# Cross-attention scores: probabilities kept as bit patterns, one maximum per half, another order on VectorE

## The chip, the cores and the metric

The kernel runs on one core of a Trainium2 chip. The metric is device time in microseconds (us) of the whole launch, and lower is better. TensorE (PE) multiplies matrices, VectorE (DVE) reduces and copies, ScalarE (ACT) does exponentials and copies, GpSimd (POOL) and SyncE (SP) do the rest. Each engine works through its own list of instructions in order and waits on semaphores that the others raise.

## The reference

One decoder layer on x of 2 x 512 tokens by 512 channels: a causal self-attention, a cross-attention to 2048 context tokens, and a mixture of 8 experts. The change touches the cross-attention, 16 heads of 32 channels, 1024 queries, 2048 keys:

```python
q = _fq_sym(q, axis=-1)
k = _fq_sym(k, axis=-1)
v = _fq_sym(v, axis=2)
attn = jnp.einsum('bhqd,bhkd->bhqk', q, k)
attn = jax.nn.softmax(attn.astype(jnp.float32), axis=-1)
attn = _fq_unsigned(attn, axis=-1)
out = jnp.einsum('bhqk,bhkd->bhqd', attn, v)
```

`_fq_unsigned` rounds every probability to one of 256 steps between 0 and the row's largest. The kernel gets those steps without a division: exp(score - largest score + log 255), rounded to an integer, is the step number, and the sum of the unrounded values gives the softmax's denominator.

## The kernel before, in words

The whole layer is one program of stages. The change is in `cross_scores` (L1178 to L1384 of the printed function) and in the type of one tile that `cross_attention` allocates.

**Units.** The work of `cross_scores` is 128 units: 8 tiles of 128 queries (`TT`) times 16 heads (`H`), head fastest. Unit n has two halves of 1024 keys, a (keys 0 to 1023) and b (keys 1024 to 2047). For each unit:

- TensorE makes the scores of a half with two matmuls of 512 columns (`scores`, L1342) into PSUM: half a into one of two buffers `cs_s_a`, half b into the one buffer `cs_s_b`.
- VectorE takes the maximum: of half a with one reduction over 1024 (`max_a`, L1301), of half b with two over 512, the first as soon as the first matmul is done (L1313). A small reduction over the three results (L1316) and a multiply-add (L1320) give the bias of the exponential, `cs_bias`.
- ScalarE does two exponentials of 1024, half b first, then a (L1287). Each writes 16-bit integers 0 to 255 to `cs_p_int`, and is followed by a short instruction that reads out the sum (ACTIVATION_READ_ACCUMULATOR).
- TensorE transposes each half in 8 blocks of 128 x 128 (L1350) into the one PSUM buffer `cs_tp`, viewing the integers as 16-bit floats. Half b goes first and is copied out by ScalarE (L1293), then half a, which is copied out by VectorE (L1328). Both copies convert the integer to a bf16 number in `cs_pT`.
- TensorE multiplies `cs_pT` by the values `v_int` in 16 matmuls of 32 columns (L1376) into `cs_out`.

**Order of the work.** It is written out by hand as one `step(t, h, n)` for each engine. TensorE's step n is: scores b of unit n (after the exponential b of unit n-1 has read `cs_s_b`), transposes b of n-1, scores a of n+1 (after exponential a of n-1), the value matmuls of n-2, transposes a of n-1. VectorE's step n is: maximum b of n, small maximum, bias of n, maximum a of n+1, copy of the transposed half a of n-1, and once a tile the copy of `cs_out` (L1332). ScalarE's step n is: exponential b, exponential a, copy of the transposed half b, all of n; at a new tile it also keeps the sums (L1270) and fetches the scales (L1280). The first 15 units and the last are unrolled, the 112 between run in a hardware loop of 16 units, seven turns.

**The table.** ScalarE's exponential needs a table. The load (ACT_TABLE_LOAD) stands just before the first exponential, behind that one's wait for the bias.

Of the kernel before, what the change touches and what calls it, by code (L numbers as in the profile page):

```python
# [6 lines left out]
F32 = mybir.dt.float32  # L7
# [25 lines left out]
QMAX = 127.0  # L33
PMAX = 255.0
LN_PMAX = log(PMAX)
Q_FLOOR = 1e-08


# [1138 lines left out]
def cross_scores(nc, k_parts, v_int, q_int, q_step, q_nstep, o_raw, z_sum, wp_dram, bp_dram, wp, ident16):  # L1177
# [10 lines left out]
    with ExitStack() as ctx:  # L1188
# [7 lines left out]
            return ctx.enter_context(nc.semaphore("cs_" + name))  # L1196

        p_int = sb("cs_p_int", [P, 2, KEYS], I16)
        pT = sb("cs_pT", [P, 2, KT, P], BF16)
        top = sb("cs_top", [P, 2, 3], F32)  # L1200
        top1 = sb("cs_top1", [P, 2], F32)


# [1 line left out]
        nstep_now = sb("cs_nstep_now", [P, H], F32)  # L1205
        z_now = sb("cs_z_now", [P, H, 2], F32)
        bias = sb("cs_bias", [P, 2], F32)
        s_a = [psum(f"cs_s_a{i}", [P, HALF], F32) for i in range(2)]
        s_b = psum("cs_s_b", [P, HALF], F32)
        tp = psum("cs_tp", [P, HKT, P], F16)  # L1210
# [55 lines left out]
        @block.scalar  # L1266
        def _(act):
            def keep_sums(t, n):
                act.wait_ge(ea_ok, n)
                nc.scalar.copy(z_sum[:, t, :, :], z_now[:, :, :]).then_inc(act_tile, 1)  # L1270
                act.wait_ge(act_tile, 2 * t + 2)

            def step(t, h, n):
                if not exists(n):
                    return
                u = h % 2
                if h == 0:
                    if at_least(n, H):
                        keep_sums(t - 1, n)
                    nc.scalar.copy(step_now[:, :], q_step[:, t, :]).then_inc(act_tile, 1)  # L1280
                    act.wait_ge(act_tile, 2 * t + 1)
                for half, s, made, used in ((1, s_b, eb_ok, tb_ok), (0, s_a[u], ea_ok, ta_ok)):
                    if half:
                        act.wait_ge(bias_ok, n + 1)
                    if at_least(n, 2):
                        act.wait_ge(used, n - 1)
                    nc.scalar.activation(p_int[:, u, half * HALF:(half + 1) * HALF], s[:, :], ACT.Exp,  # L1287
                                         bias=bias[:, u:u + 1], scale=step_now[:, h:h + 1],
                                         accum_out=z_now[:, h, half:half + 1]).then_inc(made, 1)
                act.wait_ge(tb_ok, n + 1)  # L1290
                if at_least(n, 2):
                    act.wait_ge(av_ok, n - 1)
                nc.scalar.copy(pT[:, u, HKT:KT, :], tp[:, :, :].bitcast(I16)).then_inc(rb_ok, 1)  # L1293
            units(act, step)
            keep_sums(TT - 1, UNITS)

        @block.vector
        def _(v_):
# [4 lines left out]
            def step(t, h, n):  # L1303
                u = h % 2
                if exists(n):
                    if h == 0:
# [1 line left out]
                            v_.wait_ge(bias_ok, n)  # L1308
                        nc.vector.tensor_copy(nstep_now[:, :], q_nstep[:, t, :]).then_inc(dve_tile, 1)
                        v_.wait_ge(dve_tile, t + 1)  # L1310
                    for c in range(2):
                        v_.wait_ge(sb_ok, 2 * n + c + 1)
                        nc.vector.tensor_reduce(top[:, u, 1 + c:2 + c], s_b[:, c * 512:(c + 1) * 512], AX_X,  # L1313
                                                ALU.max).then_inc(max_ok, 1)
                    v_.wait_ge(max_ok, 3 * n + 3)
                    nc.vector.tensor_reduce(top1[:, u:u + 1], top[:, u, :], AX_X, ALU.max).then_inc(top_ok, 1)  # L1316
                    v_.wait_ge(top_ok, n + 1)
                    if at_least(n, 2):
                        v_.wait_ge(ea_ok, n - 1)
                    nc.vector.tensor_scalar(bias[:, u:u + 1], top1[:, u:u + 1], nstep_now[:, h:h + 1], LN_PMAX,  # L1320
                                            ALU.mult, ALU.add).then_inc(bias_ok, 1)
                if exists(n + 1):
                    max_a(1 - u, n + 1)
                if at_least(n, 1) and exists(n - 1):
                    v_.wait_ge(ta_ok, n)
                    if at_least(n, 3):
                        v_.wait_ge(av_ok, n - 2)
                    nc.vector.tensor_copy(pT[:, 1 - u, 0:HKT, :], tp[:, :, :].bitcast(I16)).then_inc(ra_ok, 1)  # L1328
                if h == 1 and at_least(n, H):

                    v_.wait_ge(av_ok, n - 1)
                    nc.vector.tensor_copy(o_raw[:, t - 1, :], out[:, :]).then_inc(out_read, 1)  # L1332

            max_a(0, 0)
            units(v_, step)

        @block.tensor
        def _(pe):
            def scores(t, h, s, half, made, each_bank=False):
                for c in range(2):  # L1340
                    keys = half * HALF + c * 512
                    ins = nc.tensor.matmul(s[:, c * 512:(c + 1) * 512], q_int[0:3 * D, t, h, :],  # L1342
                                           k_parts[0:3 * D, h, keys:keys + 512], start=True, stop=True)
                    if each_bank or c == 1:
                        ins.then_inc(made, 1)

            def transposes(u, half, made):
                for k in range(HKT):
# [4 lines left out]
            def step(t, h, n):  # L1353
                u = h % 2
                before = at_least(n, 1) and exists(n - 1)
                if exists(n):
                    if at_least(n, 1):
                        pe.wait_ge(eb_ok, n)
                    scores(t, h, s_b, 1, sb_ok, each_bank=True)
                if before:  # L1360
                    pe.wait_ge(eb_ok, n)
                    if at_least(n, 2):
# [6 lines left out]
                if at_least(n, 2):  # L1369
# [3 lines left out]
                    if head == 0 and at_least(n, H):  # L1373
                        pe.wait_ge(out_read, t)
                    for k in range(KT):
                        ins = nc.tensor.matmul(out[:, head * D:(head + 1) * D], pT[:, u, k, :],  # L1376
                                               v_int[:, k, head * D:(head + 1) * D], start=(k == 0), stop=(k == KT - 1))
                    ins.then_inc(av_ok, 1)
                if before:
# [134 lines left out]
def cross_attention(nc, wq, bq, ctxT, wkv_in, bkv, wp, bp, v_raw, x_res, mv, rstd, ident, minus_half, ident16, ident_bf, used):  # L1514
    with ExitStack() as ctx:
# [2 lines left out]

        k_parts = sb("k_parts", [3 * D, H, KEYS], BF16)
        v_step = sb("v_step", [P, C], F32)  # L1520
        v_int = sb("v_int", [P, KT, C], BF16)

        wq_raw = v_int[:, :, :].rearrange("p t c -> p (t c)")[:, 0:2 * CK * C].bitcast(F32)\
            .rearrange("p (k c) -> p k c", k=CK)
# [774 lines left out]
```

## Time and profile before

| what | value |
|---|---|
| time, median of 3 runs (lowest, highest) | 1240.04 us (1235.86, 1241.66) |
| time of the profiled execution | 1237.78 us |
| its span in the trace | 1236.1 us |
| busy, share of the span: PE / DVE / ACT / POOL | 81% / 69% / 57% / 20% |
| `cross_scores`, first to last exponential b | 404.6 to 865.1 us |
| largest groups: L1313 DVE, L1301 DVE, L1287 ACT (two), L1350 PE | 164.8, 155.5, 154.1, 152.8, 158.4 us |

The span is from the first to the last instruction of the profiled execution, and the time of that execution is 1.7 us more. A timeline row gives the start of an instruction, its duration, engine, line, operation and tiles; where instructions of one line follow each other they are merged, with their count at the end (x8). An idle time before a row and what ended it stand in brackets. Busy PE includes the time in which a result is still on its way out of the array, so consecutive matmuls overlap in it.

### The profile page before, as it was taken

What the parts mean: (1) busy time and instruction counts of PE and PEld (TensorE: products, weight loads), DVE (VectorE), ACT (ScalarE), POOL (GpSimd) and SP (SyncE); (2) the same over time, 40 slices, a digit from 0 to 9 for tenths busy, and PEclk for the clock granted to TensorE, in tenths of its full rate; (3) what the DMA queues carried; (4) which work ended last, traced back from release to release, by engine and by line L of the source; (5) the groups of instructions that cost most, each with busy time, mean ns of one, the idle gap of its engine ahead of it and who ended that gap; (6) DMA issues with size and microseconds to landing.
All of it is one profiled execution on the core that took longest, in us unless ns stands there. A gap on an engine that the chain in (4) does not pass through costs nothing. (4 is left out here: it accounts for less than half of the span.)

```text
span 1236.1 us, 21867 instructions
## 1 busy us (share of the span) xinstructions
PE 1003.9 (81%) x8049; PEld 682.7 (55%) x8049; DVE 852.8 (69%) x1409; ACT 700.4 (57%) x1039; POOL 243.6 (20%) x216
## 2 busy tenths in 40 slices
PE   4888996999457777777777777777779989999998
PEld 3745744888345444444444444444557765556566
DVE  6857546999687899999999999999661521111126
ACT  3453362455426899999999999999223202212221
POOL 1134063556250200000000000000533610000014
PEclk9999998999678799999999999999779989999999
DMA  8200004110000000000000000000040395131215
GB/s 320 96 1 1 1 2 154 51 34 17 9 0 13 31 1 2 1 0 0 0 0 0 0 0 0 0 0 0 1 151 27 135 379 230 60 116 64 69 56 182
DMA packets 24854, 68.14 MB, mean 55 GB/s; under 512 B 2722, under 2 KB 6818, under 8 KB 23778
## 3 DMA queue, kind: packets, MB, share of 16 engines
q1 hardware_dynamic: 20114, 52.48, 11.3%
q0 software_dynamic: 4400, 14.42, 3.7%
q8 instruction: 35, 0.57, 0.2%
q10 hardware_dynamic: 288, 0.52, 0.1%
q14 instruction: 17, 0.14, 0.0%
HBM read 49.07 MB, written 18.35 MB: 55 GB/s over the span
## 5 line engine op out<-in xcount | busy, mean ns | idle before, releaser
L1313 DVE TENSOR_REDUCE cs_top<-cs_s_b 128x1 f32<-128x512 f32 x256 | 164.8, 685 | 16.7 <-PE cs_s_b L1342 7.6
L1350 PE MATMUL cs_tp<-ident,cs_p_int 128*128 128x128 f16 x2048 | 158.4, 221 | 7.5 <-ACT cs_pT L1293 2.8
L1287 ACT ACTIVATE cs_p_int<-cs_s_b,cs_bias,cs_step_now 128x1024 int16<-128x1024 f32 x128 | 154.1, 1204 | 11.6 <-DVE cs_bias L1320 5.3
L1301 DVE TENSOR_REDUCE cs_top<-cs_s_a 128x1 f32<-128x1024 f32 x128 | 155.5, 1215 | 7.2 <-PE cs_s_a L1342 7.2
L1350 PEld LDWEIGHTS cs_tp<-ident,cs_p_int 128*128 128x128 f16 x2048 | 122.1, 98 | 60.3 <-issue 45.6
L1342 PE MATMUL cs_s_b<-k_parts,q_int 96*128 96x512 bf16 x256 | 79.0, 391 | 93.4 <-ACT cs_p_int L1287 93.1
L1287 ACT ACTIVATE cs_p_int<-cs_s_a,cs_bias,cs_step_now 128x1024 int16<-128x1024 f32 x128 | 152.8, 1194 | 0.0
L1293 ACT CAST cs_pT<-cs_tp 128x1024 bf16<-128x1024 int16 x128 | 129.5, 1012 | 3.3 <-PE cs_tp L1350 2.7
L2159 PE MATMUL ff_h<-ff_experts,ff_zgT 128*128 x368 | 115.1, 467 | 1.0 <-ACT ff_zgT L1798 0.9
L1446 POOL TENSOR_TENSOR co_o<-co_o,v_step 128x512 f32<-128x512 f32 x8 | 10.7, 1331 | 467.6 <-DVE co_o L1468 467.6
L1342 PE MATMUL cs_s_a<-k_parts,q_int 96*128 96x512 bf16 x256 | 79.4, 393 | 22.9 <-ACT cs_p_int L1287 18.7
L1328 DVE CAST cs_pT<-cs_tp 128x1024 bf16<-128x1024 int16 x128 | 87.1, 680 | 4.3 <-PE cs_tp L1350 3.9
L2159 PEld LDWEIGHTS ff_h<-ff_experts,ff_zgT 128*128 128x128 f32 x368 | 69.3, 193 | 36.7 <-issue 3.3
L1376 PEld LDWEIGHTS cs_out<-v_int,cs_pT 128*128 128x128 bf16 x2048 | 70.3, 96 | 31.3 <-issue 1.1
L2052 DVE TENSOR_TENSOR ff_run_g<-ff_run_s,ff_h 128x352 f32<-128x352 f32 x23 | 12.0, 521 | 99.0 <-ACT ff_run_s L1835 82.8
L1342 PEld LDWEIGHTS cs_s_b<-k_parts,q_int 96*128 (+1 forms) x256 | 14.7, 97 | 116.6 <-ACT cs_p_int L1287 109.7
L1376 PE MATMUL cs_out<-v_int,cs_pT 128*128 128x32 bf16 x2048 | 71.4, 177 | 0.8 <-DVE cs_pT L1328 0.8
L2182 PE MATMUL ff_py<-ff_experts,ff_gT 128*128 x138 | 63.2, 593 | 0.8 <-DVE ff_gT L2016 0.8
L1835 ACT ACTIVATE ff_run_s<-ff_h 128x352 f32<-128x352 f32 x23 | 10.7, 464 | 90.4 <-PE ff_h L2159 90.4
L245 POOL TENSOR_TENSOR stage<-stage,mask 128x512 f32<-128x512 f32 x32 | 40.3, 1274 | 61.2 <-ACT stage L316 61.2
L2015 DVE COPY ff_gT<-ff_pc 128x256 f32<-128x256 f32 x23 | 9.8, 424 | 61.1 <-PE ff_pc L2170 61.1
L529 PE MATMUL sa_pj<-sa_w_hi,sa_z_hi 128*128 128x512 f32 x96 | 40.0, 417 | 7.5 <-DVE sa_y L409 3.8
(278 smaller groups left out, 2099.0 us busy)
## 6 DMA issues: line engine op xcount, KB each, us to landing
ff_experts<-in_experts_dram SPq DMA_DIRECT2D x8, 2176.0 KB, 14.6
slots<-sa_zero SPq DMA_DIRECT2D x1, 5888.0 KB, 25.8
ff_zg<-slots POOLq DMA_DIRECT2D x23, 256.0 KB, 2.9
run_y<-ff_yv SPq DMA_DIRECT2D x23, 256.0 KB, 2.0
ff_raw<-in_weights_dram SPq DMA_DIRECT2D x6, 768.0 KB, 5.8
ck_raw<-in_ctxT_dram SPq DMA_DIRECT2D x8, 512.0 KB, 3.3
stage<-in_cwkv_dram SPq DMA_DIRECT2D x2, 1024.0 KB, 6.8
out_dram<-x_res SPq DMA_DIRECT2D x8, 256.0 KB, 2.0
```

What stands on the lines that cost most here:

```text
L245: pool.tensor_tensor(diag, diag, mask[:, :].unsqueeze(1).broadcast_to([P, GH, P]), ALU.mult).then_inc(masked, 1)
L529: ins = nc.tensor.matmul(out, a(k), w[:, m, k, :], start=(k == 0 and i == 0), stop=(k == CK - 1 and i == 2))
L1287: nc.scalar.activation(p_int[:, u, half * HALF:(half + 1) * HALF], s[:, :], ACT.Exp, bias=bias[:, u:u + 1], scale=step_now[:, h:h + 1], ac ...
L1293: nc.scalar.copy(pT[:, u, HKT:KT, :], tp[:, :, :].bitcast(I16)).then_inc(rb_ok, 1)
L1301: nc.vector.tensor_reduce(top[:, u, 0:1], s_a[u][:, :], AX_X, ALU.max).then_inc(max_ok, 1)
L1313: nc.vector.tensor_reduce(top[:, u, 1 + c:2 + c], s_b[:, c * 512:(c + 1) * 512], AX_X, ALU.max).then_inc(max_ok, 1)
L1328: nc.vector.tensor_copy(pT[:, 1 - u, 0:HKT, :], tp[:, :, :].bitcast(I16)).then_inc(ra_ok, 1)
L1342: ins = nc.tensor.matmul(s[:, c * 512:(c + 1) * 512], q_int[0:3 * D, t, h, :], k_parts[0:3 * D, h, keys:keys + 512], start=True, stop=True)
L1350: ins = nc.tensor.transpose(tp[:, k, :], p_int[:, u, key:key + P].bitcast(F16), ident16[:, :])
L1376: ins = nc.tensor.matmul(out[:, head * D:(head + 1) * D], pT[:, u, k, :], v_int[:, k, head * D:(head + 1) * D], start=(k == 0), stop=(k == ...
L2159: ins = nc.tensor.matmul(out[u % 2][:, 0:I_W], zgT[:, u % 2, k, :], w, start=(k == 0), stop=(k == CK - 1))
L2182: ins = nc.tensor.matmul(py[u % 2][:, :], gT[0:rows, u % 2, j, :], w, start=(j == 0), stop=(j == DN - 1))
```

## The change

It touches `cross_scores` in seven places.

1. `cs_pT` holds the 16-bit integers as they are instead of bf16 numbers. The value matmuls view them as half-precision floats (an integer n then reads as n / 2^24), `v_int` becomes half-precision, and the copy of `cs_out` becomes a multiplication by 2^24 (`P_UNIT`).
2. ScalarE's copy of a transposed half views both sides as 32-bit integers: 512 elements instead of 1024. VectorE's copy keeps 1024 elements of 16 bits, without a conversion.
3. The maximum of half b is one reduction over 1024, which waits for both matmuls, and TensorE raises `sb_ok` once a unit.
4. The small maximum is over two numbers.
5. VectorE copies the transposed half a of n-1 before it takes the maximum of half a of n+1, not after.
6. An exponential of one column on a tile of its own stands at the head of ScalarE's list, and the table load with it.
7. The copy of `cs_out` is a `tensor_scalar` in place of a `tensor_copy`.

```diff
+P_UNIT = 2.0 ** 24
...
-        pT = sb("cs_pT", [P, 2, KT, P], BF16)
-        top = sb("cs_top", [P, 2, 3], F32)
+        pT = sb("cs_pT", [P, 2, KT, P], I16)
+        top = sb("cs_top", [P, 2, 2], F32)
...
-                nc.scalar.copy(pT[:, u, HKT:KT, :], tp[:, :, :].bitcast(I16)).then_inc(rb_ok, 1)
+                nc.scalar.copy(pT[:, u, HKT:KT, :].rearrange("p k q -> p (k q)").bitcast(I32),
+                               tp[:, :, :].rearrange("p k q -> p (k q)").bitcast(I32)).then_inc(rb_ok, 1)
+            nc.scalar.activation(table[:, :], ident16[:, 0:1], ACT.Exp)
...
-                    for c in range(2):
-                        v_.wait_ge(sb_ok, 2 * n + c + 1)
-                        nc.vector.tensor_reduce(top[:, u, 1 + c:2 + c], s_b[:, c * 512:(c + 1) * 512], AX_X,
-                                                ALU.max).then_inc(max_ok, 1)
-                    v_.wait_ge(max_ok, 3 * n + 3)
+                    v_.wait_ge(sb_ok, n + 1)
+                    nc.vector.tensor_reduce(top[:, u, 1:2], s_b[:, :], AX_X, ALU.max).then_inc(max_ok, 1)
+                    v_.wait_ge(max_ok, 2 * n + 2)
...
-                if exists(n + 1):
-                    max_a(1 - u, n + 1)
                 if at_least(n, 1) and exists(n - 1):
                     v_.wait_ge(ta_ok, n)
                     if at_least(n, 3):
                         v_.wait_ge(av_ok, n - 2)
                     nc.vector.tensor_copy(pT[:, 1 - u, 0:HKT, :], tp[:, :, :].bitcast(I16)).then_inc(ra_ok, 1)
+                if exists(n + 1):
+                    max_a(1 - u, n + 1)
                 if h == 1 and at_least(n, H):
                     v_.wait_ge(av_ok, n - 1)
-                    nc.vector.tensor_copy(o_raw[:, t - 1, :], out[:, :]).then_inc(out_read, 1)
+                    nc.vector.tensor_scalar(o_raw[:, t - 1, :], out[:, :], P_UNIT, None, ALU.mult).then_inc(out_read, 1)
...
-            def scores(t, h, s, half, made, each_bank=False):
+            def scores(t, h, s, half, made):
...
-                    if each_bank or c == 1:
-                        ins.then_inc(made, 1)
+                ins.then_inc(made, 1)
...
-                        ins = nc.tensor.matmul(out[:, head * D:(head + 1) * D], pT[:, u, k, :],
+                        ins = nc.tensor.matmul(out[:, head * D:(head + 1) * D], pT[:, u, k, :].bitcast(F16),
...
-        v_int = sb("v_int", [P, KT, C], BF16)
+        v_int = sb("v_int", [P, KT, C], F16)
```

VectorE's list in `cross_scores`, one unit in the steady state, before. `cs_s_a` and `cs_s_b` are the scores of the two halves, `cs_tp` the transposed half, and the brackets hold the semaphores that the instruction waits for.

```order
L1301 TENSOR_REDUCE cs_top<-cs_s_a 128x1 [waits cs_sa_ok]
L1328 CAST cs_pT<-cs_tp 128x1024 [waits cs_av_ok,cs_ta_ok]
L1313 TENSOR_REDUCE cs_top<-cs_s_b 128x1 [waits cs_sb_ok] x2
L1316 TENSOR_REDUCE cs_top<-cs_top 128x1 [waits cs_max_ok]
L1320 TENSOR_SCALAR cs_bias<-cs_top,cs_nstep_now 128x1 [waits cs_ea_ok,cs_top_ok]
```

The same place of the changed kernel:

```order
L1322 TENSOR_SCALAR cs_bias<-cs_top,cs_nstep_now 128x1 [waits cs_ea_ok,cs_top_ok]
L1328 COPY cs_pT<-cs_tp 128x1024 [waits cs_av_ok,cs_ta_ok]
L1305 TENSOR_REDUCE cs_top<-cs_s_a 128x1 [waits cs_sa_ok]
L1316 TENSOR_REDUCE cs_top<-cs_s_b 128x1 [waits cs_sb_ok]
L1318 TENSOR_REDUCE cs_top<-cs_top 128x1 [waits cs_max_ok]
```

The copy, with its wait for the transposes of half a (`cs_ta_ok`), now stands right behind the bias and ahead of both maxima of the next unit; the two reductions of half b are one.

ScalarE's list at the head of `cross_scores`, before:

```order
L1280 COPY cs_step_now<-q_step 128x16
L1287 ACT_TABLE_LOAD [waits cs_bias_ok]
L1287 ACTIVATE cs_p_int,cs_z_now<-cs_s_b,cs_bias,cs_step_now 128x1024 [waits cs_act_tile]
L1287 ACTIVATE cs_p_int,cs_z_now<-cs_s_a,cs_bias,cs_step_now 128x1024
L1293 CAST cs_pT<-cs_tp 128x1024 [waits cs_tb_ok]
```

And of the changed kernel:

```order
L1297 ACT_TABLE_LOAD
L1297 ACTIVATE cs_table<-ident 128x1
L1282 COPY cs_step_now<-q_step 128x16
L1289 ACTIVATE cs_p_int,cs_z_now<-cs_s_b,cs_bias,cs_step_now 128x1024 [waits cs_bias_ok,cs_act_tile]
L1289 ACTIVATE cs_p_int,cs_z_now<-cs_s_a,cs_bias,cs_step_now 128x1024
L1295 COPY cs_pT<-cs_tp 128x512 [waits cs_tb_ok]
```

The table load has moved ahead of the wait for the first bias, and the copy has half as many elements.

## Rows read from the trace of the kernel before

**Rows 1.** Window 404.5 to 865: length, busy PE, PEld, DVE, ACT, POOL, granted clock, DMA.

```profile
404.50:865.00 460.50, 343.77 (x4546) 218.69 (x4546) 432.66 (x774) 444.71 (x650) 6.40 (x2) 0.99 0.00 0
```

**Rows 2.** Timeline, one unit and its neighbours: start us, us, engine, line, operation.

```profile
499.19 1.21 DVE L1301 TENSOR_REDUCE cs_top<-cs_s_a 128x1 f32<-128x1024 f32 x1
499.31 1.20 ACT L1287 ACTIVATE cs_p_int<-cs_s_b,cs_bias,cs_step_now 128x1024 int16<-128x1024 f32 x1
500.32 0.68 DVE L1328 CAST cs_pT<-cs_tp 128x1024 bf16<-128x1024 int16 x1
500.41 0.19 ACT L1287 ACTIVATION_READ_ACCUMULATOR cs_p_int<-cs_s_b,cs_bias,cs_step_now 128x1 f32 x1
500.50 1.19 ACT L1287 ACTIVATE cs_p_int<-cs_s_a,cs_bias,cs_step_now 128x1024 int16<-128x1024 f32 x1
500.66 0.60 PE L1342 MATMUL cs_s_b<-k_parts,q_int 96*128 96x512 bf16 x2 [0.64 <-ACT cs_p_int L1287]
501.08 1.29 DVE L1313 TENSOR_REDUCE cs_top<-cs_s_b 128x1 f32<-128x512 f32 x2
501.14 0.61 PE L1350 MATMUL cs_tp<-ident,cs_p_int 128*128 128x128 f16 x8
501.79 1.01 ACT L1293 CAST cs_pT<-cs_tp 128x1024 bf16<-128x1024 int16 x1
501.93 0.60 PE L1342 MATMUL cs_s_a<-k_parts,q_int 96*128 96x512 bf16 x2 [0.18 <-ACT cs_p_int L1287]
502.37 0.56 PE L1376 MATMUL cs_out<-v_int,cs_pT 128*128 128x32 bf16 x16
502.41 0.16 DVE L1316 TENSOR_REDUCE cs_top<-cs_top 128x1 f32<-128x3 f32 x1
502.60 0.21 DVE L1320 TENSOR_SCALAR cs_bias<-cs_top,cs_nstep_now 128x1 f32<-128x1 f32 x1
502.73 1.21 DVE L1301 TENSOR_REDUCE cs_top<-cs_s_a 128x1 f32<-128x1024 f32 x1
502.85 1.20 ACT L1287 ACTIVATE cs_p_int<-cs_s_b,cs_bias,cs_step_now 128x1024 int16<-128x1024 f32 x1
502.94 0.61 PE L1350 MATMUL cs_tp<-ident,cs_p_int 128*128 128x128 f16 x8
```

**Rows 3.** Groups of instructions: count, busy us, mean ns of one, idle before it.

```profile
L1313 DVE TENSOR_REDUCE cs_top<-cs_s_b 128x1 f32<-128x512 f32 x256 | 164.8, 685 | 16.7 <-PE cs_s_b L1342 7.6
L1301 DVE TENSOR_REDUCE cs_top<-cs_s_a 128x1 f32<-128x1024 f32 x128 | 155.5, 1215 | 7.2 <-PE cs_s_a L1342 7.2
L1328 DVE CAST cs_pT<-cs_tp 128x1024 bf16<-128x1024 int16 x128 | 87.1, 680 | 4.3 <-PE cs_tp L1350 3.9
L2015 DVE COPY ff_gT<-ff_pc 128x256 f32<-128x256 f32 x23 | 9.8, 424 | 61.1 <-PE ff_pc L2170 61.1
L1293 ACT CAST cs_pT<-cs_tp 128x1024 bf16<-128x1024 int16 x128 | 129.5, 1012 | 3.3 <-PE cs_tp L1350 2.7
L1798 ACT COPY ff_zgT<-ff_pc 128x512 f32<-128x512 f32 x23 | 13.5, 585 | 37.7 <-PE ff_pc L2147 37.7
```

**Rows 4.** Instructions of L1287: durations ns, then first and last start us.

```profile
L1287 ACT ACTIVATE cs_p_int<-cs_s_b,cs_bias,cs_step_now x128: 1203/1203/1211, 404.6 to 865.1; 128x1024 int16<-128x1024 f32 x128
```

**Rows 5.** Timeline at the stage's start, ScalarE.

```profile
403.26 1.28 ACT L1287 ACT_TABLE_LOAD   x1 [4.03 <-DVE cs_bias L1320]
```

**Rows 6.** Timeline, VectorE, two instructions that follow with no gap.

```profile
642.56 0.68 DVE L1332 COPY stage<-cs_out 128x512 f32 x1
643.16 0.68 DVE L1313 TENSOR_REDUCE cs_top<-cs_s_b 128x1 f32<-128x512 f32 x1
```

**Rows 7.** Timeline near the stage's start, ScalarE, first exponential of two consecutive units.

```profile
408.74 1.21 ACT L1287 ACTIVATE cs_p_int<-cs_s_b,cs_bias,cs_step_now 128x1024 int16<-128x1024 f32 x1
412.92 1.21 ACT L1287 ACTIVATE cs_p_int<-cs_s_b,cs_bias,cs_step_now 128x1024 int16<-128x1024 f32 x1
```

**Rows 8.** Window 408 to 412, same columns as Rows 1; granted clock 0.50.

```profile
408.00:412.00 4.00, 3.56 (x21) 1.99 (x20) 3.42 (x6) 3.22 (x5) 3.32 (x1) 0.50 0.00 0
```

More of the change, by code:

```diff
@@ L1207, in cross_scores @@
         bias = sb("cs_bias", [P, 2], F32)
+        table = sb("cs_table", [P, 1], F32)
         s_a = [psum(f"cs_s_a{i}", [P, HALF], F32) for i in range(2)]
@@ L1358, in step @@
                         pe.wait_ge(eb_ok, n)
-                    scores(t, h, s_b, 1, sb_ok, each_bank=True)
+                    scores(t, h, s_b, 1, sb_ok)
                 if before:
```

## The prediction

> **What bounds the kernel now.** I read the windows first: the change touches only the stretch from 404.5 to 865 us, and there VectorE is busy 432.66 of 460.5 us and ScalarE 444.71, TensorE 343.77 with gaps [rows 1]. Two engines near their limit do not say which one sets the pace, so the timeline comes next. From one exponential b (499.31) to the next (502.85) a unit takes 3.54 us [rows 2]. The instruction view gives 128 of them, first start 404.6, last 865.1 [rows 4]: 127 intervals of 3.63 us on average. The 0.09 us over 3.54 (11 us in all) are the slow first units and the edges between query tiles.
>
> Which wait ends last? There is one buffer for the scores b, and this loop goes through it: exponential b starts at 499.31; its sum is read out by 500.60 (500.41 + 0.19); scores b of the next unit start at 500.66; their first half is reduced from 501.08; the two reductions last 1.29 and the small one starts at 502.41; bias at 502.60; exponential b at 502.85 [rows 2]. No link has slack of more than 0.06 us. A second loop is as long to within a few hundredths: transposes b end at 501.75 (501.14 + 0.61), ScalarE's copy starts at 501.79 and ends at 502.80, and exponential b follows at 502.85 [rows 2]. So the cheaper ScalarE copy alone cannot shorten a unit.
>
> **The change, part by part.** I count on a clock whose 0 is the start of exponential b of unit n-1 (499.31 in rows 2).
>
> *One maximum for half b.* Before, VectorE started at 1.77 (501.08), while the second matmul was still running. Now it waits for both, which end at 501.26 (500.66 + 0.60), and with the 0.04 us that the other dependent starts show, starts at 1.99. The one reduction should last 1.215, as the one of the same shape over half a does, against 1.29 for the pair [rows 2, 3]. The small maximum starts at 1.99 + 1.215 + 0.04 = 3.245 and not at 3.10 (502.41). The loop through scores b becomes 3.54 + 0.145 = 3.69 us. VectorE has less to do, but the loop is longer, because an overlap with the second matmul was worth more than the start-up that is saved.
>
> *Three numbers to two in the small maximum.* Nothing: its 0.16 us are start-up [rows 2].
>
> *The copy ahead of the maximum of half a.* VectorE now meets the wait for transposes a of n-1 right after the bias of n. When is that transpose done? TensorE's chain does not move: exponential a ends, scores a start at 2.62 (501.93), value matmuls at 3.06, transposes a at 3.63 (502.94), end 4.24 [rows 2]. The bias of n starts at 3.245 + 0.19 = 3.44, so VectorE stands idle from 3.65 to 4.28. Before, the maximum of half a (1.21 us) filled exactly this hole: it started at 502.73, and the copy behind it found its transposes done [rows 2]. Behind the waiting copy now stand maximum a and maximum b of the next unit. Copy starts at 4.28; the next instruction 0.60 later, as behind a copy of 0.68 us in rows 6; maximum a at 4.88; maximum b 1.13 later (499.19 to 500.32 in rows 2), at 6.01; its end 7.225; small maximum 7.265; bias 7.455; exponential b of n+1 0.25 later, at 7.705. That is two units, so the new loop is 3.85 us a unit, longer than the 3.69, and it decides. Difference to 3.54: 0.31 us, and over 127 intervals 39.5 us.
>
> *ScalarE's copy.* From 1012 ns to about 585, by the row of a PSUM copy of 512 four-byte elements [rows 3]. It starts after the sum of exponential a is read (2.48) and ended at 3.49; transposes a wait for it, but also for the value matmuls, which end at 3.62. So even the old 1012 ns would be covered; nothing in the steady state. At the tile edges ScalarE does two extra copies behind which the exponential waits; its new slack may take back part of the 11 us above. I put 2 us there, with 0 and 5 as ends.
>
> *VectorE's copy without a conversion.* Same 1024 elements of 16 bits from PSUM; I keep 680 ns [rows 3]. Ends: 424 ns, the row of a copy of a quarter of the elements at four bytes [rows 3], which would put the two-unit loop at 7.45, 3.72 a unit, and 1215 ns, the row of 1024 elements at one element a step, which would put it at 8.24, 4.12 a unit.
>
> *Half-precision value matmuls.* I keep 0.56 us for 16. As an upper bound I take the time of the transposes, which are half-precision with 4 times the columns (0.61 for 8, so about 0.9 at most for 16 at their pitch): 0.3 later for transposes a, 0.17 us a unit, 21 us. Below: no gain, since nothing about them gets smaller.
>
> *The copy of the output as a multiplication*, 8 times, stays one pass over 512 elements of PSUM (0.68 us, rows 6), now behind maximum a: nothing, give or take 0.1 us each.
>
> *Table load.* 1.28 us stood between the first bias and the first exponential [rows 5]; ScalarE was idle 4.03 us before it, and the load now fits into that. Gain 1.3 us, once.
>
> **Sum:** 39.5 - 2 - 1.3 = 36 us on the profiled execution's 1237.8, which is 1274. That execution lies 2.3 us under the median of the three runs (1240.04), so for a median I say 1275.
>
> **A rule against a row.** VectorE's instructions overlap a little here: behind the 0.68 us copy the next starts after 0.60 [rows 6], behind a 1.21 us maximum after 1.13 [rows 2]. My chain uses these. The Trainium skill, "VectorE: DVE Perf Modes", section "The DRAIN you can't avoid", says that the next instruction does not start until the pipeline is empty. Taken strictly it would add 0.08 us twice in two units, 0.08 a unit, and 10 us to the sum: 1285 (2 in 100, which the forecast's chance below includes). The rows here have the instructions starting before the recorded end of the one in front, so I go by the rows.
>
> **The rivals.**
>
> - *Only the merged maximum counts* (12 in 100). If transposes a were done earlier than I read, or the copy were as short as its lower end, the loop of 3.69 would decide: 0.145 x 127 = 18.5, less 1.3, so +17, 1256. For it: the ends of matmuls are modelled in the trace. Against it: ScalarE's copy follows the recorded end of transposes b by 0.04, so that end is about right.
> - *Faster* (9 in 100). The loop through scores b is shorter, not longer: if the second matmul's result can be reduced as early as the first's, 0.22 us before its recorded end, the one reduction (1.215 for 1.29) takes 0.075 off each unit, and with the table that is 11 us: 1227. It decides only if transposes a too end 0.6 us earlier than the row says, by 3.65, when the bias ends; otherwise VectorE's wait for them costs more. For it: VectorE and ScalarE do 0.15 and 0.43 us less in each unit, and both are over 90% busy. Against it: both would have to be recorded late.
> - *No change that can be measured* (4 in 100): a mixture, where the merged maximum costs some and the edges give it back. Half a per cent, 6 us, is about what can be told from nothing here.
> - *VectorE's copy drops to one element a step* (4 in 100): 4.12 a unit, 0.58 x 127 = 74, less 3: 1309.
> - *TensorE's clock falls* (3 in 100). The granted clock is 0.99 over the stretch, but 0.50 in 408 to 412 [rows 1, 8], which is the 1.2 GHz level, and there a unit took 4.18 us (408.74 to 412.92) [rows 7]. The change lengthens TensorE's pauses, from 0.65 us ahead of scores b to about 1.0. If the low level stayed for the whole stage, 0.64 us a unit over the old pace would come on top: 1274 + 81 = 1355. The Trainium skill, "TensorE: Matmul & The Clock Gate", section "The HAM clock gate", has the gate follow how busy TensorE has been; by that rule a slower unit carries this risk. The busy share falls only from 0.75 to about 0.69, so I think it stays high.
>
> **How the numbers follow.** The forecast (3.85 a unit, 1275, with 1265 to 1295 for the unknown copy, matmuls and edges) has 68 in 100. The range takes in the merged-only case and the upper bound of the matmuls: 1251 to 1294; outside are the faster case, no change, and the two dear ones, 20 in 100 together. Slower by over 0.5%: 68 + 12 + 4 + 3 = 87. Within: 4. Faster: 9.
>
> **What would show it.** Exponential b every 3.85 us with VectorE's copy waiting about 0.6 us a unit for TensorE's transposes (about 75 us in all, against 3.9 before [rows 3]); one reduction over half b of 1215 ns starting about 0.65 after scores b start; ScalarE's copy at about 585 ns and ScalarE's busy share down. It would be wrong if VectorE's copy had no wait, if the unit were 3.69 or less, or if the copy's duration had moved.

## The result, and the profile after

| | before | changed |
|---|---|---|
| median, us (lowest, highest) | 1238.67 (1235.86, 1241.66) | 1271.03 (1266.98, 1274.62) |
| span of the profiled execution, us | 1236.1 | 1272.9 |

Four runs of each. The changed kernel is slower: ratio 1.0272, 95% interval 1.0230 to 1.0315. That is 32.4 us by the medians (a quotient of 1.026, inside the interval), in the forecast range, 4 us under the predicted 1275. The predicted difference was 35 us on a median of 1240; a fourth run of the kernel before has moved that median to 1238.67.

The stage first. The instruction view of the exponential, with first and last start of the 128 exponentials b:

```profile
L1289 ACT ACTIVATE cs_p_int<-cs_s_b,cs_bias,cs_step_now x128: 1204/1204/1206, 403.2 to 902.6; 128x1024 int16<-128x1024 f32 x128
```

The interval is 902.6 - 403.2 over 127, or 3.93 us a unit, against 3.63 before [rows 4]. It is 38.9 us longer in all, and the span is 36.8 us longer: the difference lies in this stage. The first exponential starts 1.3 us earlier than before (403.2, not 404.6), with the first bias at 402.94 here and 402.96 there.

The groups of the profile page that answer to [rows 3] (columns as there: count, busy us, mean ns, idle before and its releaser):

```profile
L1289 ACT ACTIVATE cs_p_int<-cs_s_b,cs_bias,cs_step_now 128x1024 int16<-128x1024 f32 x128 | 154.2, 1204 | 100.7 <-DVE cs_bias L1322 100.7
...
L1316 DVE TENSOR_REDUCE cs_top<-cs_s_b 128x1 f32<-128x1024 f32 x128 | 155.8, 1217 | 7.9 <-PE cs_s_b L1344 7.5
...
L1328 DVE COPY cs_pT<-cs_tp 128x1024 int16<-128x1024 int16 x128 | 88.3, 690 | 57.5 <-PE cs_tp L1351 57.5
...
L1295 ACT COPY cs_pT<-cs_tp 128x512 int32<-128x512 int32 x128 | 75.0, 586 | 12.4 <-PE cs_tp L1351 11.7
```

VectorE's copy kept its length (690 ns, before 680), and has 57.5 us of waiting for the transposes where it had 3.9. ScalarE's copy takes 586 ns, as the copy of 512 words in [rows 3] said, and ScalarE now waits 100.7 us for the bias. The merged maximum takes 1217 ns.

The timeline of two units of the changed kernel, in the place of [rows 2] (start us, us, engine, line, operation, idle before and releaser):

```profile
501.25 1.20 ACT L1289 ACTIVATE cs_p_int<-cs_s_b,cs_bias,cs_step_now 128x1024 int16<-128x1024 f32 x1 [0.82 <-DVE cs_bias L1322]
501.51 0.69 DVE L1328 COPY cs_pT<-cs_tp 128x1024 int16<-128x1024 int16 x1 [0.30 <-PE cs_tp L1351]
...
502.60 0.60 PE L1344 MATMUL cs_s_b<-k_parts,q_int 96*128 96x512 bf16 x2 [1.12 <-ACT cs_p_int L1289]
...
503.04 0.61 PE L1351 MATMUL cs_tp<-ident,cs_p_int 128*128 128x128 f16 x8
503.25 1.22 DVE L1316 TENSOR_REDUCE cs_top<-cs_s_b 128x1 f32<-128x1024 f32 x1
...
503.69 0.59 ACT L1295 COPY cs_pT<-cs_tp 128x512 int32<-128x512 int32 x1
...
503.87 0.60 PE L1344 MATMUL cs_s_a<-k_parts,q_int 96*128 96x512 bf16 x2 [0.22 <-ACT cs_p_int L1289]
...
504.31 0.56 PE L1377 MATMUL cs_out<-v_int,cs_pT 128*128 128x32 f16 x16
504.50 0.15 DVE L1318 TENSOR_REDUCE cs_top<-cs_top 128x1 f32<-128x2 f32 x1
504.69 0.21 DVE L1322 TENSOR_SCALAR cs_bias<-cs_top,cs_nstep_now 128x1 f32<-128x1 f32 x1
...
504.71 0.61 PE L1351 MATMUL cs_tp<-ident,cs_p_int 128*128 128x128 f16 x8
504.94 1.20 ACT L1289 ACTIVATE cs_p_int<-cs_s_b,cs_bias,cs_step_now 128x1024 int16<-128x1024 f32 x1 [0.66 <-DVE cs_bias L1322]
505.36 0.69 DVE L1328 COPY cs_pT<-cs_tp 128x1024 int16<-128x1024 int16 x1 [0.46 <-PE cs_tp L1351]
505.97 1.21 DVE L1305 TENSOR_REDUCE cs_top<-cs_s_a 128x1 f32<-128x1024 f32 x1
...
507.10 1.22 DVE L1316 TENSOR_REDUCE cs_top<-cs_s_b 128x1 f32<-128x1024 f32 x1
...
508.54 0.21 DVE L1322 TENSOR_SCALAR cs_bias<-cs_top,cs_nstep_now 128x1 f32<-128x1 f32 x1
508.79 1.20 ACT L1289 ACTIVATE cs_p_int<-cs_s_b,cs_bias,cs_step_now 128x1024 int16<-128x1024 f32 x1 [0.82 <-DVE cs_bias L1322]
```

Read it from the exponential b at 501.25. Scores b start 1.35 later (502.60), as before. The maximum of half b waits for both matmuls and starts at 503.25, 0.65 after them. The copy starts only at 505.36, after 0.46 us of idling until the transposes of half a are done (504.71 + 0.61). The maximum of half a follows 0.61 later, maximum b at 507.10, 1.13 after that, and the exponential b of the unit after next at 508.79. Two units take 7.54 us, 3.77 each, and they are not alike: 3.69 (501.25 to 504.94) and 3.85 (504.94 to 508.79). The copy waits in both, 0.30 and 0.46.

3.77 is less than the 3.85 of the forecast, yet the mean is 3.93. The windows show what else there is. The window from 420 to 850 us, before, then changed (length, then busy us of PE, PEld, DVE, ACT, POOL, then the granted clock, DMA share, GB/s):

```profile
420.00:850.00 430.00, 320.11 (x4273) 203.81 (x4269) 406.39 (x727) 416.29 (x610) 0.00 (x0) 1.00 0.00 0
```

```profile
420.00:850.00 430.00, 294.73 (x3937) 197.26 (x3936) 369.22 (x560) 334.79 (x562) 0.00 (x0) 0.93 0.00 0
```

The granted clock fell from 1.00 to 0.93: about a seventh of the stretch is at the 1.2 GHz level. One such place, the matmuls of TensorE behind a long pause (timeline, columns as above):

```profile
475.00 0.60 PE L1344 MATMUL cs_s_b<-k_parts,q_int 96*128 96x512 bf16 x2 [1.73 <-ACT cs_p_int L1289]
...
476.27 1.03 PE L1344 MATMUL cs_s_a<-k_parts,q_int 96*128 96x512 bf16 x2 [0.22 <-ACT cs_p_int L1289]
```

A pair of matmuls of 512 columns takes 0.60 us before the clock falls and 1.03 after. From 477 to 481 us the granted clock is 0.50. The long pause comes with the tile edge, the step from one tile of 128 queries to the next, where VectorE also copies `cs_out`. In the changed kernel each of the seven edges has a stretch at the low level behind it, within two units.

The tile edges themselves can be read where the clock is high. Exponential b just ahead of an edge, and the one four units later, before:

```profile
455.57 1.20 ACT L1287 ACTIVATE cs_p_int<-cs_s_b,cs_bias,cs_step_now 128x1024 int16<-128x1024 f32 x1
...
470.98 1.20 ACT L1287 ACTIVATE cs_p_int<-cs_s_b,cs_bias,cs_step_now 128x1024 int16<-128x1024 f32 x1 [0.46 <-DVE cs_bias L1320]
```

And of the changed kernel:

```profile
457.57 1.20 ACT L1289 ACTIVATE cs_p_int<-cs_s_b,cs_bias,cs_step_now 128x1024 int16<-128x1024 f32 x1 [0.66 <-DVE cs_bias L1322]
...
473.64 1.21 ACT L1289 ACTIVATE cs_p_int<-cs_s_b,cs_bias,cs_step_now 128x1024 int16<-128x1024 f32 x1 [1.42 <-DVE cs_bias L1322]
```

Four units around an edge take 15.41 us before, 1.25 over four plain ones of 3.54, and 16.07 in the changed kernel, 0.99 over four of 3.77. The edges give back 0.26 us each, 1.8 us over seven.

### The profile page after: what moved, and what is told of

The parts are those of the page before. It is cut to its first block and busy times, and to the rows that moved or that the text cites. A ratio compares the mean times of both kernels' runs of the same rounds, so it can differ in the third digit from the quotient of the medians.

```text
span 1272.9 us, 21523 instructions
## 1 busy us (share of the span) xinstructions
PE 1001.9 (79%) x8049; PEld 692.4 (54%) x8049; DVE 846.4 (66%) x1281; ACT 643.4 (51%) x1040; POOL 244.1 (19%) x216
## 5 line engine op out<-in xcount | busy, mean ns | idle before, releaser
L1289 ACT ACTIVATE cs_p_int<-cs_s_b,cs_bias,cs_step_now 128x1024 int16<-128x1024 f32 x128 | 154.2, 1204 | 100.7 <-DVE cs_bias L1322 100.7
L1344 PE MATMUL cs_s_b<-k_parts,q_int 96*128 96x512 bf16 x256 | 85.3, 418 | 135.6 <-ACT cs_p_int L1289 135.2
L1351 PE MATMUL cs_tp<-ident,cs_p_int 128*128 128x128 f16 x2048 | 170.1, 231 | 2.6 <-ACT cs_p_int L1289 1.4
L1316 DVE TENSOR_REDUCE cs_top<-cs_s_b 128x1 f32<-128x1024 f32 x128 | 155.8, 1217 | 7.9 <-PE cs_s_b L1344 7.5
L1351 PEld LDWEIGHTS cs_tp<-ident,cs_p_int 128*128 128x128 f16 x2048 | 138.0, 103 | 40.3 <-issue 12.8
L1328 DVE COPY cs_pT<-cs_tp 128x1024 int16<-128x1024 int16 x128 | 88.3, 690 | 57.5 <-PE cs_tp L1351 57.5
L1344 PE MATMUL cs_s_a<-k_parts,q_int 96*128 96x512 bf16 x256 | 85.2, 418 | 23.6 <-ACT cs_p_int L1289 18.7
L1377 PEld LDWEIGHTS cs_out<-v_int,cs_pT 128*128 128x128 f16 x2048 | 72.2, 98 | 35.3 <-issue 9.6
L1295 ACT COPY cs_pT<-cs_tp 128x512 int32<-128x512 int32 x128 | 75.0, 586 | 12.4 <-PE cs_tp L1351 11.7
L1377 PE MATMUL cs_out<-v_int,cs_pT 128*128 128x32 f16 x2048 | 72.7, 179 | 0.8 <-DVE cs_pT L1328 0.8
## 6 DMA issues: line engine op xcount, KB each, us to landing
ff_experts<-in_experts_dram SPq DMA_DIRECT2D x8, 2176.0 KB, 15.5
```

Source lines behind the costliest of these rows:

```text
L1295: nc.scalar.copy(pT[:, u, HKT:KT, :].rearrange("p k q -> p (k q)").bitcast(I32), tp[:, :, :].rearrange("p k q -> p (k q)").bitcast(I32)).t ...
L1316: nc.vector.tensor_reduce(top[:, u, 1:2], s_b[:, :], AX_X, ALU.max).then_inc(max_ok, 1)
L1351: ins = nc.tensor.transpose(tp[:, k, :], p_int[:, u, key:key + P].bitcast(F16), ident16[:, :])
```

## The experiments

All are compared with the kernel before, run on the same chip beside them; between experiments compare the ratio with its interval, since they ran on different chips. "Unit" is the interval between exponentials b; "clock" is the granted clock from 420 to 850 us, and "at the full clock" means units in which it was 1.00.

### One maximum, nothing else

```diff
-                    for c in range(2):
-                        v_.wait_ge(sb_ok, 2 * n + c + 1)
-                        nc.vector.tensor_reduce(top[:, u, 1 + c:2 + c], s_b[:, c * 512:(c + 1) * 512], AX_X,
-                                                ALU.max).then_inc(max_ok, 1)
+                    v_.wait_ge(sb_ok, n + 1)
+                    nc.vector.tensor_reduce(top[:, u, 1:2], s_b[:, :], AX_X, ALU.max).then_inc(max_ok, 1)
```

> The kernel before with only the single maximum of half b. My theory (the loop through the one score buffer is 3.54 + 0.145 a unit, since VectorE loses its overlap with the second matmul): one exponential b every 3.69 to 3.70 us, 16 to 20 us slower than before, and VectorE's copy of the transposed half waits for nothing. Rival A (the merged maximum saves start-up on an engine that is over 90% busy): at or under 3.54 a unit, 0 to 10 us faster. Rival B (the merged maximum is the whole of the loss): as slow as the changed kernel, about 32 us over before.

Measured: 1254.39 us against 1234.76, ratio 1.0146 (1.0110 to 1.0181), 19.6 us. The timeline of this kernel, one unit:

```profile
599.71 1.20 ACT L1287 ACTIVATE cs_p_int<-cs_s_b,cs_bias,cs_step_now 128x1024 int16<-128x1024 f32 x1 [0.21 <-DVE cs_bias L1318]
...
601.06 0.60 PE L1340 MATMUL cs_s_b<-k_parts,q_int 96*128 96x512 bf16 x2 [0.81 <-ACT cs_p_int L1287]
...
601.70 1.23 DVE L1312 TENSOR_REDUCE cs_top<-cs_s_b 128x1 f32<-128x1024 f32 x1 [0.30 <-PE cs_s_b L1340]
...
602.96 0.15 DVE L1314 TENSOR_REDUCE cs_top<-cs_top 128x1 f32<-128x2 f32 x1
603.15 0.21 DVE L1318 TENSOR_SCALAR cs_bias<-cs_top,cs_nstep_now 128x1 f32<-128x1 f32 x1
...
603.40 1.20 ACT L1287 ACTIVATE cs_p_int<-cs_s_b,cs_bias,cs_step_now 128x1024 int16<-128x1024 f32 x1 [0.20 <-DVE cs_bias L1318]
```

The second matmul ends at 601.66 and the maximum starts at 601.70; before, the first reduction started 0.42 after the scores, here 0.64. The small maximum comes 1.90 after the scores (602.96), before 1.75 (501.08 + 1.29 + 0.04 against 500.66 in [rows 2]). The unit is 3.69. This is the predicted loop, and both rivals are out: the merged maximum loses time alone, and it is not the whole loss.

### The copy first, nothing else

```diff
-                if exists(n + 1):
-                    max_a(1 - u, n + 1)
                 if at_least(n, 1) and exists(n - 1):
                     v_.wait_ge(ta_ok, n)
...
+                if exists(n + 1):
+                    max_a(1 - u, n + 1)
```

> The kernel before with only VectorE's copy moved ahead of the maximum of half a. My theory (behind the copy's wait for the transposes stand both maxima, a loop over two units): 3.83 to 3.90 us a unit, 30 to 42 us slower than before, VectorE's copy waiting 0.4 us or more in most units for TensorE's transposes. It should be slower than the whole change, because ScalarE's old copy of 1012 ns still holds the transposes back and the two reductions of half b cost VectorE more than the one. Rival (the order is harmless and the merged maximum is the loss): within 6 us of before.

Measured: 1306.72 us, ratio 1.0576 (1.0539 to 1.0614), 72 us slower. The direction is right and so is the comparison with the whole change, but the size is twice what I wrote. Exponentials b in a stretch at the full clock (timeline of ScalarE):

```profile
827.71 1.21 ACT L1287 ACTIVATE cs_p_int<-cs_s_b,cs_bias,cs_step_now 128x1024 int16<-128x1024 f32 x1
...
831.90 1.21 ACT L1287 ACTIVATE cs_p_int<-cs_s_b,cs_bias,cs_step_now 128x1024 int16<-128x1024 f32 x1 [0.74 <-DVE cs_bias L1320]
...
835.45 1.21 ACT L1287 ACTIVATE cs_p_int<-cs_s_b,cs_bias,cs_step_now 128x1024 int16<-128x1024 f32 x1
...
839.63 1.20 ACT L1287 ACTIVATE cs_p_int<-cs_s_b,cs_bias,cs_step_now 128x1024 int16<-128x1024 f32 x1 [0.73 <-DVE cs_bias L1320]
```

The two-unit loop is there: 827.71 to 835.45 is 7.74, 3.87 a unit, as expected. It splits into 4.19 and 3.55. The rest is in the window from 420 to 850:

```profile
420.00:850.00 430.00, 319.03 (x3683) 209.90 (x3681) 352.20 (x627) 356.26 (x525) 0.00 (x0) 0.83 0.00 0
```

The clock is 0.83 here: a third of the stretch at 1.2 GHz. At the full clock the loop is worth 0.33 x 127 = 42 of the 72 us; 30 are not the loop. That asked for an experiment of its own, further down.

### The formats and the table, with the old list on VectorE

The changed kernel with both edits of VectorE's list undone.

> Everything of the change but the two edits of VectorE's list: bit patterns in place of converted numbers, half-precision values, ScalarE's copy of 512 words, early table; two maxima for half b and the old order. My theory: the loop through the one score buffer stays at 3.54 a unit and decides, so only the table (1.3 us) and some of the tile edges are gained: 1 to 6 us faster than before; transposes a start about 0.40 us after the value matmuls where they started 0.57 after, since ScalarE's copy no longer holds them. Rival A (ScalarE's copy was half of the pace): 3.4 a unit or less, 15 us or more faster. Rival B (the half-precision matmuls or the copies cost time): over 3.6 a unit, 8 us or more slower than before.

Measured: 1231.18 us against 1234.76, ratio 0.9959 (0.9942 to 0.9975), 3.6 us faster, the expected size. The timeline:

```profile
500.31 1.20 ACT L1289 ACTIVATE cs_p_int<-cs_s_b,cs_bias,cs_step_now 128x1024 int16<-128x1024 f32 x1 [0.47 <-DVE cs_bias L1324]
...
502.79 0.59 ACT L1295 COPY cs_pT<-cs_tp 128x512 int32<-128x512 int32 x1
...
503.36 0.56 PE L1380 MATMUL cs_out<-v_int,cs_pT 128*128 128x32 f16 x16
...
503.77 0.61 PE L1354 MATMUL cs_tp<-ident,cs_p_int 128*128 128x128 f16 x8
```

The transposes of half a start 0.41 after the value matmuls (503.36, 503.77), not 0.57 as in [rows 2]; ScalarE's copy ended at 503.38, far from holding them. Half-precision matmuls take 0.56 us for 16, as the bf16 ones did. The unit stays at 3.54 for most units, because the loop through the one score buffer is untouched: 0.43 us less work on ScalarE in each unit buys next to nothing. The gain of 3.6 us is of the size of two things together: the table (1.3) and the second unit of each tile edge, 3.67 us where it was 4.09 (2.9 over seven edges). This version has the lowest ratio of all that ran, and is faster than both kernels of the comparison.

### The changed kernel with the old order

> The changed kernel with the old order on VectorE (maximum a ahead of the copy). My theory: the merged maximum's loop is left, 3.69 to 3.70 us a unit at the full clock, 12 to 20 us slower than before, so 12 to 20 us faster than the changed kernel; the granted clock of the stretch goes back to 0.97 or more as TensorE's pauses shorten. Rival (the order is harmless): within 5 us of the changed kernel.

(The edit is the one of "the copy first", reversed, on the changed kernel.) Measured: 1250.21 us against 1234.76, ratio 1.0112 (1.0076 to 1.0148), 15.5 us slower. As expected, and the clock is back at 0.99:

```profile
420.00:850.00 430.00, 294.61 (x4144) 189.13 (x4143) 386.31 (x589) 354.49 (x590) 0.00 (x0) 0.99 0.00 0
```

So with the old order the whole change costs 1.1%, and the new order adds the other 1.6%.

### The changed kernel with two maxima

The reverse of the first edit, on the changed kernel.

> The changed kernel with two maxima for half b again; the copy still ahead of the maximum of half a. Theory (VectorE's copy waits for the transposes, and behind it everything that VectorE does for half b counts): the two reductions cost VectorE 0.07 us more than the one where its own work is the loop, so 3.77 to 3.83 us a unit at the full clock: as slow as the changed kernel or a few us slower, 28 to 45 us over before. So the merged maximum costs 16 to 20 us in the old order and nothing in the new. Rival (the two losses add up): 12 us or more faster than the changed kernel.

Measured: 1291.75 us against 1241.51, ratio 1.0403 (1.0337 to 1.0469), 50 us. Worse than the 28 to 45 expected. At the full clock the pace is what was expected: exponentials b at 839.82, 843.45 and 847.42, so 3.63 and 3.97, 7.60 for two units and 3.80 each. What came on top is the clock again:

```profile
420.00:850.00 430.00, 302.56 (x3813) 202.53 (x3812) 363.68 (x648) 323.87 (x542) 0.00 (x0) 0.88 0.00 0
```

The rival, that the losses add up, is out with the opposite sign: the merged maximum costs 1.5% under the old order and, going by 1.0272 against 1.0403, saves about 1.3% (16 us) under the new one. Of these 16, the pace at the full clock explains 0.03 x 127 = 4 (7.54 against 7.60 for two units). The other 12 go with the higher clock.

### The changed kernel with ScalarE's wide copy

```diff
-                nc.scalar.copy(pT[:, u, HKT:KT, :].rearrange("p k q -> p (k q)").bitcast(I32),
-                               tp[:, :, :].rearrange("p k q -> p (k q)").bitcast(I32)).then_inc(rb_ok, 1)
+                nc.scalar.copy(pT[:, u, HKT:KT, :], tp[:, :, :].bitcast(I16)).then_inc(rb_ok, 1)
```

> The changed kernel with ScalarE's copy as 1024 elements of 16 bits again. Theory: that copy (about 1012 ns) ends behind the value matmuls and holds the transposes of half a 0.17 us longer, which VectorE's copy waits for, so the unit goes from 3.77 to about 3.84 at the full clock: 8 us or more over the changed kernel, more if the low clock grows. Rival (as in the prediction: the copy's length is covered): within 3 us of the changed kernel.

Measured: 1298.89 us against 1242.81, ratio 1.0460 (1.0428 to 1.0493), 1.8% over the changed kernel where the prediction had nothing. The clock, 420 to 850:

```profile
420.00:850.00 430.00, 322.00 (x3744) 213.19 (x3742) 350.25 (x532) 361.76 (x531) 0.00 (x0) 0.83 0.00 0
```

The exponentials b at the full clock:

```profile
841.23 1.20 ACT L1289 ACTIVATE cs_p_int<-cs_s_b,cs_bias,cs_step_now 128x1024 int16<-128x1024 f32 x1 [0.24 <-DVE cs_bias L1321]
...
845.21 1.20 ACT L1289 ACTIVATE cs_p_int<-cs_s_b,cs_bias,cs_step_now 128x1024 int16<-128x1024 f32 x1 [0.52 <-DVE cs_bias L1321]
...
848.90 1.20 ACT L1289 ACTIVATE cs_p_int<-cs_s_b,cs_bias,cs_step_now 128x1024 int16<-128x1024 f32 x1 [0.24 <-DVE cs_bias L1321]
```

Two units take 7.67 us, 3.84 each, as expected, against 7.54 with the short copy. So under the new order the short copy is worth 0.065 x 127 = 8 us at the full clock, because it holds the transposes less long and VectorE's copy waits for those. All in all it is worth some 20 us; the rest goes with the clock, 0.83 against 0.93.

### Extra work for TensorE, to test the clock

```diff
                     transposes(1 - u, 0, ta_ok)
+                if at_least(n, 2) and exists(n) and h != 1:
+                    cols = (h - 1) % H * D
+                    for k in range(KT):
+                        nc.tensor.matmul(out[:, cols:cols + D], q_int[0:3 * D, t, h, :],
+                                         k_parts[0:3 * D, h, k * D:(k + 1) * D], start=True, stop=True)
```

On the changed kernel:

> The changed kernel with 16 extra matmuls of 32 columns on TensorE behind the transposes of half a, in 112 + 6 or so of the 128 units, whose result nobody reads (it is overwritten by the value matmuls). They fall into TensorE's pause ahead of the scores b and lengthen no chain at the full clock. Theory (the changed kernel's stretches at 1.2 GHz, 76 us of the stage, come with its longer pauses and cost 8 to 10 us): low stretches shrink to 30 us or less and the time falls by 5 to 10 us against the changed kernel, to about 25 us over before; the unit at the full clock stays at 3.77. Rival (the low clock does not depend on these pauses, or costs nothing): the same low stretches and the same time within 3 us, or slower as TensorE has more to do.

Measured: 1265.89 us against 1242.81, ratio 1.0182 (1.0164 to 1.0201). The changed kernel had 1.0272, so adding useless work makes it 0.9% faster, 11 us by the ratios and 9 by the medians, and the clock goes from 0.93 to 0.99:

```profile
420.00:850.00 430.00, 324.50 (x5704) 240.28 (x5705) 378.05 (x574) 340.76 (x573) 0.00 (x0) 0.99 0.00 0
```

At the full clock the units keep their 3.69 and 3.84 (exponentials b at 501.55, 505.25 and 509.09), and a low stretch follows three of the seven tile edges, not all. So the gain is not a shorter loop.

On "the copy first":

> The kernel before with VectorE's copy moved ahead of the maximum of half a, and the same extra matmuls of 32 columns, whose result nobody reads. Without them that kernel came out 72 us slower than before, where its loops at the full clock give 3.83 to 3.90 us a unit, 35 us; 181 us of its stage were at the 1.2 GHz level. Theory (the other half is the clock): with the extra matmuls the low stretches shrink to under 60 us and the time falls by 20 to 35 us. Rival (the order alone costs it): the same 72 us or more.

Measured: 1291.27 us against 1242.81, ratio 1.0395 (1.0370 to 1.0420), against 1.0576 without: 1.8%, some 22 us, at a clock of 0.96 where it was 0.83. That is most of the 30 us that the loop did not explain:

```profile
420.00:850.00 430.00, 334.33 (x5496) 244.42 (x5494) 369.23 (x656) 373.54 (x550) 0.00 (x0) 0.96 0.00 0
```

On the kernel before, as a control:

> The kernel before with the same 16 extra matmuls of 32 columns a unit, whose result nobody reads. A control: theory (they fall into a pause of 0.65 us and before has hardly any low clock to win back): within 4 us of before, the unit still 3.54 us. Rival (the extra matmuls win or cost time by themselves): 5 us or more either way, and then the two runs with them on the changed order must be read by that much less or more.

Measured: 1240.20 us against 1241.51, ratio 0.9991 (0.9975 to 1.0007). The unit is still 3.54 and the clock 1.00. The extra matmuls are free where the clock is high already, and win nothing that can be told from the noise there. So what they win in the other two is the clock.

### Splitting the exponential of half b

Three exponentials a unit, each half of b freeing its own bank of scores:

```diff
-                for half, s, made, used in ((1, s_b, eb_ok, tb_ok), (0, s_a[u], ea_ok, ta_ok)):
+                for first, last, s, made, used, part in ((HALF, HALF + 512, s_b[:, 0:512], eb_ok, tb_ok, 1),
+                                                         (HALF + 512, KEYS, s_b[:, 512:HALF], eb_ok, None, 2),
+                                                         (0, HALF, s_a[u][:, :], ea_ok, ta_ok, 0)):
...
+                    if n is not None:
+                        pe.wait_ge(eb_ok, 2 * n - 1 + c)
```

> The formats and the early table of the change, two maxima for half b, the old order on VectorE, and the exponential of half b as two of 512, each of which frees its bank of scores for the next unit's matmul (the sums get a third column). Theory (the loop through the one score buffer is what sets the pace of the kernel before): that loop falls to about 3.3, VectorE's own work of about 3.4 becomes the bound, ScalarE has 3.35: 3.40 to 3.45 a unit, 10 to 20 us faster than before. Rival (the pace was set by VectorE's or ScalarE's work already, and ScalarE gets 0.35 us more of it): no faster than the formats alone, which were 3.6 us under before, or slower.

Measured: 1239.82 us against 1242.81, ratio 0.9977 (0.9965 to 0.9988). A miss: no faster than the formats alone, whose ratio was 0.9959. The timeline, from the first part of one unit's exponential b over two units:

```profile
523.90 0.78 ACT L1291 ACTIVATE cs_p_int<-cs_s_b,cs_bias,cs_step_now 128x512 int16<-128x512 f32 x1 [0.89 <-DVE cs_bias L1326]
...
526.52 0.20 ACT L1291 ACTIVATION_READ_ACCUMULATOR cs_p_int<-cs_s_a,cs_bias,cs_step_now 128x1 f32 x1
...
526.86 0.60 PE L1350 MATMUL cs_s_a<-k_parts,q_int 96*128 96x512 bf16 x2 [0.43 <-ACT cs_p_int L1291]
...
527.27 0.78 ACT L1291 ACTIVATE cs_p_int<-cs_s_b,cs_bias,cs_step_now 128x512 int16<-128x512 f32 x1
...
527.50 1.22 DVE L1307 TENSOR_REDUCE cs_top<-cs_s_a 128x1 f32<-128x1024 f32 x1 [0.27 <-PE cs_s_a L1350]
...
530.99 0.78 ACT L1291 ACTIVATE cs_p_int<-cs_s_b,cs_bias,cs_step_now 128x512 int16<-128x512 f32 x1 [0.29 <-DVE cs_bias L1326]
```

This unit takes 3.37 us, as hoped, but the next takes 3.72, and 7.09 for two is no less than twice 3.54 (the mean over all units, 400.8 to 859.4, is 3.61). Exponential a now ends later, so do the scores a behind it (526.86), and VectorE stands idle 0.27 us until they are done. Its waits for them come to 23.6 us in all, where they were 7.2 [rows 3]. One loop was opened and another, over two units through half a, took its place. My expectation had left that one out.

## Why the prediction was right, and where it was not

**What bounds the kernel before: right.** The loop through the one buffer of scores b is the bound. Another loop lies close behind: with this one opened, two units still took 7.09 us. The formats alone cut ScalarE's work by 0.43 us a unit and left the unit at 3.54; the merged maximum alone, which cuts VectorE's work but lengthens that loop, took it to 3.69.

**One maximum for half b: right**, 0.145 us a unit, shown alone (19.6 us) and with the rest under the old order (15.5 us).

**The copy ahead of maximum a: right in its mechanism.** VectorE's copy idles for the transposes, both maxima stand behind it, and the loop spans two units. The copy's wait was put at 0.6 us in every unit, 75 us in all; it is 0.30 and 0.46 by turns at the full clock, and 57.5 in all. The 0.46 is the forecast's 0.63 less the error of the next point.

**ScalarE's copy: the step that failed.** The prediction said "even the old 1012 ns would be covered; nothing in the steady state". It took the value matmuls to be busy for 0.57 us, from 502.37 to the transposes at 502.94 in [rows 2]. The transposes can start 0.40 after them (504.31 to 504.71 in the changed kernel, 503.36 to 503.77 in the formats-only one), ahead of their recorded end: the other 0.17 before was the wait for ScalarE's copy, which ended at 502.80. Before the change this cost nothing, since nobody waited for the transposes of half a; the moved copy does. Two units take 7.54 and not 7.705, so 0.165 / 2 x 127 = 10 us of the forecast are missing. The run with the wide copy, 7.67, shows 0.13 of the 0.165 by itself; the last 0.03 has no run of its own.

**The clock: a rival given 3 in 100, which came about in part.** I judged that the high level would stay, and put nothing for the clock into the sum. It went to 0.93. The extra matmuls win back 9 to 11 us, and that is about what the low stretches cost. The two errors are of one size and opposite sign, so that the total came out close by luck. At the full clock alone it would be 0.23 x 127 = 29.2, less 1.8 for the edges and 1.3 for the table: 26 us, or 1266 as a median, still in the range but 9 us under the forecast. With the clock it is 35 to 37 us, where the profiled execution is 36.8 us longer and the medians 32.4 apart. The four runs of the changed kernel fit this: 1274.6 us at a granted clock of 0.929 over the whole span, 1267.0 at 0.943.

**The table: right**, 1.3 us: from the first bias to the first exponential 0.31 us (402.94 to 403.25), before 1.60 (402.96 to 404.56). **VectorE's copy and half-precision matmuls: right** to 0.01 us. **The tile edges: right**, 1.8 us where 2 were put.

**The strict reading of the pipeline rule: not what happens.** The copy of 0.69 us is followed by the next instruction after 0.61 (505.36, 505.97), in the changed kernel as in [rows 6]. The Trainium skill, "VectorE: DVE Perf Modes", section "The DRAIN you can't avoid", adds to its rule that an instruction that is not held starts earlier; the trace agrees with that sentence.

## What to carry to other kernels

A busy share over 90% on two engines did not say which loop was the bound: follow one unit from an instruction to its next occurrence, and count what is on that path. An engine's list is also a set of waits: an instruction moved ahead puts its wait in front of everything behind it, and a copy whose length was covered before is covered no longer once somebody waits for its successor. When the longer unit leaves TensorE longer pauses, read its granted clock too, since the unit at the full clock is then only part of the loss. Splitting a reduction can be worth its start-up cost when the first part overlaps the producer.

## What the runs showed of the hardware that was not expected

**A slower unit may cost twice.** Between 420 and 850 us the granted clock was 0.99 to 1.00 in the kernels with the copy last, and 0.93, 0.88, 0.83 and 0.83 in the four with the copy first and no extra work. It goes with the mean unit at the full clock, half of two neighbours:

| kernel | two neighbouring units, us | mean unit, us | granted clock |
|---|---|---|---|
| before | 3.54, 3.54 | 3.54 | 1.00 |
| split exponential | 3.37, 3.72 | 3.54 | 0.99 |
| one maximum | 3.69, 3.69 | 3.69 | 0.99 |
| changed | 3.69, 3.85 | 3.77 | 0.93 |
| changed, two maxima | 3.63, 3.97 | 3.80 | 0.88 |
| changed, wide copy | 3.69, 3.98 | 3.84 | 0.83 |
| copy first | 3.55, 4.19 | 3.87 | 0.83 |

How even the units are does not order the clock: those of the split exponential differ by 0.35 us and it keeps 0.99, while those of the wide copy differ by 0.29 and it has 0.83. So with the copy first a loss at the full clock brought a second one with it, from some 10 us in the changed kernel to 30 in the copy first. That a longer mean unit is the cause is argued from this order; that extra matmuls in the pauses raise the clock and win time (1.8% and 0.9%), and do neither where it is high already, is shown. The Trainium skill, "TensorE: Matmul & The Clock Gate", section "The HAM clock gate", says that the gate follows how busy the engine has been; these runs agree (0.93 and 0.83 rose to 0.99 and 0.96 with the extra matmuls).

**Small half-precision values multiply at full pace.** The probabilities as bit patterns are n / 2^24 with n up to 255, and 16 value matmuls took 0.56 us with them as with bf16 numbers (502.37 in [rows 2], 504.31 above).
